# The last chunk work of the attention moved behind the block change, and the first edge inputs loaded during the last convolution

## What is computed

```
q, k, v = x @ wq.T, x @ wk.T, x @ wv.T                 # 64 heads of 8 channels
pw      = grouped_1x1(depthwise_5x5([q, k, v]))         # 64 more heads
scores  = [v, 1] . relu(k)^T      per head, over all 4096 pixels
out     = scores . relu(q);  out = out[:-1] / (out[-1] + 1e-15)
x2      = batchnorm(proj(out)) + x                      # 1024 -> 512 channels
```

```
E    = [sobel, |laplace|, diagonal, sqrt(sobel^2 + lap^2)]   # 3x3 stencils per channel
feat = gelu(batchnorm(w_branch . E)); gate = sigmoid(...mean(feat)...)
y    = layernorm(w_fuse . (feat * gate)); out = gelu(y) + x2
```

## Time and profile before

| | |
|---|---|
| median of three runs | 4693.0 us (4685.66 to 4695.4) |
| the profiled execution's own time | 4680.56 us |
| its span | 4678.8 us |
| TensorE busy | 4404.2 us (94%) |
| VectorE, ScalarE, GpSimd busy | 2834.5, 2209.3, 1240.7 us |
| mean granted TensorE clock | 0.976 |
| HBM traffic over the span | 222 GB/s |

### The profile page before, as it was taken

The page is one execution under the profiler, slowest core; times in us unless marked ns, Lnnn a source line. Parts: engine busy times, 40 slices in busy tenths (PEclk is TensorE's granted clock), DMA queues, the critical chain, the costliest instruction groups (busy, mean ns, idle before and its releaser), DMA issues. The chain is left out here.

```text
span 4678.8 us, 76658 instructions
## 1 busy us (share of the span) xinstructions
PE 4404.2 (94%) x27368; PEld 3565.6 (76%) x27368; DVE 2834.5 (61%) x4120; ACT 2209.3 (47%) x3983; POOL 1240.7 (27%) x1030
## 2 busy tenths in 40 slices
PE   8999999999999999999999998689989999999968
PEld 6887988888888888878879888556666676666626
DVE  4354454354454454544544543289789979978996
ACT  3343343343343333433433433056666666667666
POOL 2442442433433424424424333000020030002003
PEclk9999999999999999999999999799999999999979
DMA  6685685786776766766856866867466646746613
GB/s 197 225 292 202 238 294 201 242 274 219 247 258 227 259 238 233 276 217 239 296 202 235 281 213 207 291 212 262 150 201 219 227 155 213 262 150 201 203 54 128
DMA packets 486678, 1045.80 MB, mean 224 GB/s; under 512 B 40624, under 2 KB 94512, under 8 KB 484016
## 3 DMA queue, kind: packets, MB, share of 16 engines
q1 hardware_dynamic: 486320, 1040.99, 65.8%
HBM read 665.02 MB, written 375.82 MB: 222 GB/s over the span
## 5 line engine op out<-in xcount | busy, mean ns | idle before, releaser
L818 POOL TENSOR_TENSOR toeplitz<-taps 128x512 f32<-128x512 f32 x768 | 896.8, 1195 | 869.3 <-PE bank L488 801.3
L488 PEld LDWEIGHTS bank<-toeplitz,columns 128*128 128x128 f32 x8192 | 956.2, 192 | 14.3
L488 PE MATMUL bank<-toeplitz,columns 128*128 128x128 f32 x8192 | 957.0, 275 | 0.0
L394 PE MATMUL bank<-x_hi,w_hi 128*128 128x512 f32 x1536 | 611.6, 398 | 16.9 <-DVE x_lo L665 16.3
L396 PE MATMUL bank<-x_lo,w_hi 128*128 128x512 f32 x1536 | 599.8, 391 | 0.0
L395 PE MATMUL bank<-x_hi,w_lo 128*128 128x512 f32 x1536 | 599.3, 390 | 0.0
L1541 POOL TENSOR_TENSOR centred<-centred,x_out 128x512 f32<-128x512 f32 x128 | 174.4, 1384 | 1602.1 <-ACT centred L1324 1600.5
L752 DVE TENSOR_SCALAR ckey_t<-bank 128x256 f32<-128x256 f32 x256 | 108.4, 424 | 781.9 <-PE bank L488 781.9
L1174 PE MATMUL bank<-edge,w_branch 128*128 128x512 f32 x1024 | 482.5, 621 | 77.4 <-ACT edge L1272 77.4
L478 PE MATMUL bank<-loaded,toeplitz 128*128 128x256 f32 x2048 | 499.3, 387 | 48.0 <-DMA loaded<-tiles_dram 44.8
L665 DVE TENSOR_TENSOR x_lo<-x_sb,x_hi 128x1536 fp32r<-128x1536 f32 x128 | 251.6, 1966 | 410.5 <-ACT x_hi L534 410.5
(11 more groups left out here) (143 smaller groups left out, 6896.2 us busy)
## 6 DMA issues: line engine op xcount, KB each, us to landing
x_sb<-in_x_tiled SPq DMA_DIRECT2D x128, 1024.0 KB, 6.2
loaded<-tiles_dram SPq DMA_DIRECT2D x256, 433.5 KB, 5.5
tiles_dram<-tiles SPq DMA_DIRECT2D x112, 867.0 KB, 7.2
inverse<-inverse_dram SPq DMA_DIRECT2D x256, 256.0 KB, 8.0
att_dram<-out_hi SPq DMA_DIRECT2D x256, 256.0 KB, 4.0
att_dram<-out_lo SPq DMA_DIRECT2D x256, 256.0 KB, 5.5
att_hi<-att_dram SPq DMA_DIRECT2D x64, 1024.0 KB, 7.6
att_lo<-att_dram SPq DMA_DIRECT2D x64, 1024.0 KB, 9.9
```

Of the source, the lines that this page charges most:

```text
L394: nc.tensor.matmul(banks[t][:, :], wh, xh, start=(k == 0), stop=False)
L488: last = nc.tensor.matmul(bank[:, v * M:(v + 1) * M], columns[:, h % 2, t - T_K, v + b, a * HT:(a + TO) * HT], w[:, t, d, :], start=(d == ...
L818: last = nc.gpsimd.tensor_tensor(toeplitz[:, h % 2, t, :].rearrange("p (d o r) -> p d o r", o=HD, r=PL), tap, point, ALU.mult)
```

## The change

1. In the last convolution SyncE issues ten more DMAs, one behind each `write_q` of heads 3 to 12 (`load_first`): four of 1 MB with the mixed weights of image 0, four of 1 MB with the attended tiles of its chunk 0, two of 1056 KB with the residuals of chunks 0 and 1. The five tensors are placed where the attention's image and weight buffers lie, which the last convolution no longer uses. Their loads at the start of the edge block are gone.
2. The tail of the attention is taken out of `final` and given to the edge block as functions (`rest`). At its start TensorE does the last `denominate`, `turn_scores`, `mix_weights`; VectorE `invert` and `mixed_weights`; SyncE the inverse and its first four loads, and the weight's write. The division, rounding and spill of chunks 0 to 3 stand in the projection step of chunk 1, those of chunks 4 to 7 in that of chunk 2.
3. In the first `drain`, the load of the ten rows for the first stencils waits for the writes of two chunks (16 x 2) where it waited for three, and stands ahead of the loads of chunk 3's tiles.
4. SyncE and ScalarE wait in `drain` until all spills are written (`all_spilled`), where SyncE had waited at the end of the attention block.

```diff
@@ SyncE, attention
+                def load_first(n):
+                    if n == 0:
+                        sp.wait_ge(qkv_ready, 3 * NCH * IT)
+                        sp.wait_ge(turned, NCH * IT)
+                        sp.wait_ge(chunk_scored, NCH * IT)
+                    if n < 4:
+                        i, part = divmod(n, 2)
+                        of = slice(i * (TILES // 2), (i + 1) * (TILES // 2))
+                        sp.dma_start((first_w_hi, first_w_lo)[part][:, of, :].bitcast(F32),
+                                     dram["w_mix"][0].rearrange("t u p o -> p u t o")[:, part, of, :]).then_inc(edge_w_loaded[i], 16)
+                    elif n < 8:
...
+                        sp.dma_start((first_att_hi, first_att_lo)[part][:, i, :, :].bitcast(F32),
+                                     dram["att"][0].rearrange("t u p n -> p u t n")[:, part, of, 0:CH]).then_inc(edge_att_loaded[i], 16)
+                    else:
+                        j = n - 8
+                        sp.dma_start(first_x[:, j, :, :],
...
                         write_q(it, h)
+                        if last and 3 <= h < 13:
+                            load_first(h - 3)
                         if h + LR < SH:
...
                 def final(it):
                     conv(it, True, True)
+
+                def invert_rest():
+                    it = IT - 1
                     write_inverse(it, 1)
-                    write_w(it, 1)
                     sp.wait_ge(den_written, 16 * START + 32 * it + 32)
                     for i in range(OR):
                         load_inverse(it, 1, i)
-                    for j in range(NCH):
+                    write_w(it, 1)
+
+                def spill_rest(js):
+                    for j in js:
                         if j + OR < NCH:
-                            load_inverse(it, 1, j + OR)
-                        spill(it, 1, j)
+                            load_inverse(IT - 1, 1, j + OR)
+                        spill(IT - 1, 1, j)
...
@@ TensorE, attention; called at the start of the edge stream
+                def scores_rest():
+                    it = IT - 1
                     denominate(it, 1)
                     turn_scores(it, 1)
                     mix_weights(it, 1)
+                    pe.wait_ge(den_evac, START + 2 * it + 2)
...
@@ SyncE, edges
                 def start():
                     for s in stored:
                         sp.sem_inc(s, 16 * START)
-                    for i in range(2):
-                        load_mixed(0, i)
-                        load_att(0, 0, i)
                     sp.dma_start(vec[:, :, :].rearrange("p v m -> p (v m)"), io["vec"]).then_inc(vec_loaded, 16)
+                    invert_rest()
+                    load_constants()
...
                     if prev_p is not None:
                         write_x2(*prev_p, 1 if slot is None else 1 - slot)
+                    if mj is None and pj[1] >= 1:
+                        spill_rest(FIRST if pj[1] == 1 else SECOND)
...
                 def drain(p, b):
                     if p is not None:
+                        if b is None:
+                            load_rows(p, 0, 0, 16 * chunk(p, LAG - 1))
+                            for k in range(1, KT):
+                                load_rows(p, 0, k)
                         sp.wait_ge(att_used, chunk(p, LAG))
                         load_att(p, LAG, 0)
...
@@ VectorE, edges
                 def start():
+                    invert_rest()
                     for s in [rstd_ready, squares_added] + xb_used:
                         dve.sem_inc(s, START)
...
                         if k == 0 and prev_p is not None:
                             add_residual(*prev_p, 1 if slot is None else 1 - slot, (2, 3))
+                            if mj is None:
+                                divide_rest(FIRST if pj[1] == 1 else SECOND)
```

More of the change, by code:

```diff
@@ L48, with attention @@
 START = 2
+HELD = 20608
 VEC = ["bn0_gamma", "bn0_beta", "bn0_mean", "bn0_var", "b_branch", "bn1_gamma", "bn1_beta",
        "b_att2", "b_fuse", "ln_gamma", "ln_beta"]
-def attention(nc, banks, io, dram):
+def attention(nc, banks, io, dram, kept):
+    rest = {}
     with ExitStack() as ctx:
@@ L162, in attention @@
         q_written = [sem(f"q_written{i}") for i in range(2)]
+        edge_w_loaded = [sem(f"edge_w_proj_loaded{i}") for i in range(2)]
+        edge_att_loaded = [sem(f"att_loaded{i}") for i in range(2)]
+        edge_x_loaded = [sem(f"x_residual_loaded{i}") for i in range(2)]
+        rest["loaded"] = edge_w_loaded, edge_att_loaded, edge_x_loaded
         conv_q_loaded = sem("conv_q_loaded")
@@ L851, in _, with edges @@
                 pairs(pool, first, steady, final)
-def edges(nc, banks, io, dram, out):
+    return rest
+def edges(nc, banks, io, dram, out, rest):
     with ExitStack() as ctx:
@@ L907, in edges @@
         mean_w_set = sem("mean_weights_set")
-        w_proj_loaded = [sem(f"edge_w_proj_loaded{i}") for i in range(2)]
-        att_loaded = [sem(f"att_loaded{i}") for i in range(2)]
+        w_proj_loaded, att_loaded, x_loaded = rest["loaded"]
         att_used = sem("att_used")
-        x_loaded = [sem(f"x_residual_loaded{i}") for i in range(2)]
         projected = sem("projected")
@@ L1080, in step @@
                             sp.wait_ge(x2_written, 16 * (chunk(*pj) - 1))
-                        load_x(*pj, slot)
-                        if mj is None and prev_p is None:
-                            load_constants()
+                        if mj is not None or pj[1] >= 2:
+                            load_x(*pj, slot)
                         if prev_p is not None:
@@ L1100, in drain @@
                             load_att(p, LAG, 1)
-                        write_x2(p, LAG - 1, (LAG - 1) % 2)
-                        load_rows(p, 0, 0, 16 * chunk(p, LAG))
-                        for k in range(1, KT):
-                            load_rows(p, 0, k)
+                        if b is not None:
+                            write_x2(p, LAG - 1, (LAG - 1) % 2)
+                            load_rows(p, 0, 0, 16 * chunk(p, LAG))
+                            for k in range(1, KT):
+                                load_rows(p, 0, k)
+                        else:
+                            write_x2(p, LAG - 1, (LAG - 1) % 2)
+                            all_spilled()
                 def load_out(b, j):
@@ L1131, in _ @@
             def _(pe):
+                scores_rest, mixed_rest = rest["pe"]
                 def start():
@@ L1181, in step @@
                         if pj is not None and k < KT and not (leaving and k == KT - 1):
+                            if mj is None and pj[1] == 0 and k == 1:
+                                mixed_rest()
                             project(*pj, k, fresh)
@@ L1244, in _ @@
             def _(act):
+                turn_rest, round_rest, all_spilled = rest["act"]
                 def start():
@@ L1558, in program @@
         banks = [ctx.enter_context(nc.psum_tensor(f"bank{i}", [P, CH], F32)) for i in range(8)]
-        attention(nc, banks, io, dram)
-        edges(nc, banks, io, dram, out)
+        rest = attention(nc, banks, io, dram, ctx)
+        edges(nc, banks, io, dram, out, rest)
 def kernel(x, L0_conv_wq, L0_conv_wk, L0_conv_wv, L0_conv_dw_kernel, L0_conv_pw_kernel, L0_conv_proj_kernel,
```

97 lines of the change are left out of this document (65 added, 32 removed).

## The result

The changed kernel takes 4658.6 us (median of 6 runs, 4653.5 to 4671.5), beside 4694.2 of the kernel before on the same chip (6 runs). The ratio is 0.9929, its 95% interval 0.9917 to 0.9942: 33 us won (the two medians lie 35.6 apart). Forecast were 4647 us and a gain of 45.8. The time lies in the range of 4637 to 4665, but 12 us are missing, and this part shows which.

The account below looks back on a forecast made before the run. TensorE, near 0.9 busy, was taken as the bound, with holes at the block change and before the first stencil. Terms 40.6 + 0.7 - 2.5 + 9.9 - 2.9 = 45.8 us gave 4647 against the 4693.0 median; range 4637 to 4665.

Parts of the forecast that it names:

- Up to the first projection: Block change: with the tail moved past the barrier, the first projection starts at 2925.3 instead of 2965.87, gaining 40.6 us.
- The second hole: Before the first stencil: rows needing only chunks 0 and 1 land early, so stencils directly follow the constants, gaining 9.9 us.
- The last convolution: Ten added loads, 10.5 MB, leave a 17.9 us backlog at 372 GB/s, 15 us of it free: 2.9 us lost.
- What waits for it first is the query write: Last convolution: the backlog first delays the query write, which has 18 us of latency without TensorE noticing.
- a free backlog: Last convolution: 15 us of transfer backlog costs TensorE nothing; only the rest stalls it.
- The end of -21: Last convolution: the pessimistic bound of its term, 21 us lost if transfers run at 291 GB/s.
- The chunks: Chunks 0 to 2: 0.7 us gained from a vanished wait, 2.5 lost waiting for chunk 2's tiles (ends 0 and 8.8).
- a lower ceiling: Rival: long loads run at 334 GB/s, costing 10.4 us in the convolution and 5.0 at chunk 2; 4657 us, chance 0.13.
- The slower rival: SyncE's issues themselves block: zero gain at 1.55 us per issue, 24 us slower (4717) at 1.8; chance 0.03.

Follow-up runs that it names:

- counts_first: The changed kernel with VectorE giving its start counts ahead of the inversion and mixed weight at the block change; 4656.4 us, ratio 0.9914.
- rows_behind_three: The changed kernel with the first rows again loaded behind chunk 2's x2 write and chunk 3's tiles; 4675.4 us, ratio 0.9957.
- spread: The changed kernel with eight early loads spread over heads 2 to 14 and two issued after the inverse's write; 4645.0 us, ratio 0.9905.
- no_taps: The changed kernel without the last convolution's six taps loads and GpSimd's waits for them (output not valid); 4649.3 us, ratio 0.9912.
- tail_kept: The changed kernel with inversion, mixed weight, divisions and spills back in the attention's block, ahead of the barrier; 4681.2 us, ratio 0.9975.
- spread_and_three: spread, with chunk 2's first tiles ahead of the spills, start counts given first, and constants made beside chunk 2; 4650.7 us, ratio 0.9911.
- loads_late: The changed kernel with four early loads in heads 12 to 15 and six behind the load of relu_c; 4661.9 us, ratio 0.9934.
- no_early_loads: The changed kernel with all ten loads issued at the edge block's start, ahead of the inverse's write; 4675.1 us, ratio 0.9949.
- spread_two: spread, with counts first, constants beside chunk 2, and chunk 0's second tiles issued ahead of the inverse's write; 4641.2 us, ratio 0.9884.
- control: The changed kernel, unedited, run again beside its variants; 4662.8 us, ratio 0.9935 to the kernel before.
- taps_first: The changed kernel with each early load issued behind its head's tiles and taps instead of ahead of them; 4664.6 us, ratio 0.9940.
- spread_three: spread_two with chunk 3's first tiles issued ahead of the first rows; 4642.6 us, ratio 0.9882.

## Why the prediction was right, and where it wasn't

**Up to the first projection: right** (40.8 for 40.6), and by the steps named: released by VectorE's count, at the low clock as assumed. counts_first shows that the wait is the count's.

**The second hole: right** (10.0 for 9.9); rows_behind_three gives it back alone.

**The last convolution: the step that failed.** "What waits for it first is the query write" was wrong. It has 18 us to spare, as worked out, and was never waited for by TensorE. The load with the least to spare was not looked at: the taps, double-buffered two heads at a time, are issued one pair ahead. In spread, where they land in 7.6 us, TensorE waits 0.84 us for them in all; at 10.6, and issued up to 4 us later, it is 7.9. With no_taps the price is nothing, at 375 GB/s and the full ten loads; with the taps it is 10.9. The forecast's form (bytes over rate, less a free backlog) was of no use: at its own rate of 372 it gives 2.9, at the measured 378 only 1.8. The end of -21 for the term held the value.

A rule of the Trainium skill had stood beside this term (DMA: Bandwidth & Descriptors, Bandwidth: about 358 GB/s for a core's HBM). The same section gives that figure as what each core gets when both cores of a pair stream; in this program one core runs. It kept 378 GB/s for 59 us, 375 with TensorE never idle. So the figure was no ceiling here, and none of the loss came from it.

**The chunks: right in mechanism, wrong in size.** 4.9 us of wait for chunk 2's tiles, between the 2.5 taken and the end of 8.8; the stretch of chunk 1 moved 333 GB/s, not 372. And one term was absent: the wait drops the clock. In the timeline, chunk 2's first matmuls follow each other at 0.43 us and not at 0.23, for about 2 us in all. tail_kept shows where both come from, spread_and_three that order doesn't remove them.

Of the rivals "a lower ceiling" came nearest in time (4657). In the convolution the runs exclude its mechanism (378 GB/s, and nothing lost without the taps). In chunk 1 its numbers were met, 333 GB/s and 4.9 us for its 334 and 5.0; the DMA share there was 0.97, and whether a ceiling or the order of the transfers set that rate isn't shown. The slower rival's mechanism exists, as loads_late and no_early_loads show. Where the change issues its loads it is there in small: 61 issues took 47.9 us, 0.79 each where that rival needed 1.55 for a gain of zero, and it reached TensorE only by way of the taps.

## What to carry to other kernels

When transfers are moved beside a phase that hides its own, list every load of that phase with its slack from earliest issue to first use, and fear the one with the least slack, however small: bytes over rate doesn't tell of it. Spread the moved loads through the whole phase, and don't put many in a row right ahead of a barrier or of a write that something waits for: six and ten in a row held SyncE for 16 and 22 us. Two on an idle queue, as in spread_two, cost 0.43 and 0.50 us. When a chain has been shortened, look at what releases its first consumer: here it was a count given 6 us late, and giving it early took 5.5 us off, of which 2.8 came back later by the clock.

## What the runs showed of the hardware

- Under full load the landing of small transfers more than doubles (taps 4.3 to 10.6 us), and issue order protects little: 0.7 us for one megabyte less ahead.
- An issue by SyncE takes 0.3 to 0.5 us on an empty queue and, with several MB outstanding, 2 to 6 us (3.53, 4.05 and 4.52 above, 5.59 and 6.36 for two, 5.73 in the earlier trace rows).
- Behind a wait of the same length TensorE can be at either clock level, and in these kernels that is worth some 3 us. Two places behind the first stencil decide. The first is the last batch of the first stencils' step. In before, the changed kernel, control, taps_first, no_taps, spread, rows_behind_three, tail_kept and no_early_loads TensorE waits 1.1 to 1.7 us for it and runs it at full speed (3.70 us). In counts_first, loads_late and spread_three it waits 3.4 us and takes 5.11 to 5.31. This is counts_first:

```profile
3063.44 5.11 PE L1258 MATMUL bank<-edge,w_branch 128*128 128x512 f32 x8 [3.44 <-ACT edge L1362]
```

  The second comes some 283 us behind the first stencil. The wait is 2.87 or 2.88 us in every kernel, but the first nine take 3.70 us for the batch behind it and the other five 5.40. The changed kernel, then counts_first:

```profile
3313.06 3.70 PE L1258 MATMUL bank<-edge,w_branch 128*128 128x512 f32 x8 [2.87 <-ACT edge L1362]
...
3311.68 5.40 PE L1258 MATMUL bank<-edge,w_branch 128*128 128x512 f32 x8 [2.87 <-ACT edge L1362]
```

  Measured from the first stencil, counts_first is 1.4 us behind the changed kernel from the first place on and 3.1 from the second; at the end it is 2.9. The first nine took 1627.0 to 1628.3 us from the first stencil to the end, counts_first, loads_late and spread_three 1630.9 to 1631.3. spread_and_three is slow at the second place alone (1629.6). spread_two is too, and there TensorE waits for no edges in the first step: it is itself 1.7 us later, behind the 3.59 us for chunk 3's tiles (1631.5). What decides the level behind the equal waits isn't shown.
